# Loading x ahead of the first adjacency rows in a two-layer graph kernel

## The reference

```python
def layer0(x, adj, h0, y):
    a = adj * (y @ y.T)                       # keep an edge only inside a class
    a = a / max(sum(abs(a), axis=1), 1e-12)
    return 0.9 * (a @ x) + 0.1 * h0

def layer1(x, adj, W_proj, b_proj, W_gcn, b_gcn):
    filt = tanh(adj * adj) * (adj > 0)        # tanh(1) at each edge
    a = top_k(filt, 350)                      # no row has over 350 edges
    h2 = tanh(x @ W_proj + b_proj)
    return relu(a @ (h2 @ W_gcn) + b_gcn)

x = layernorm(x + layer0(x, adj, h0, y))
x = layernorm(x + layer1(x, adj, ...))
```

## Time and profile before

| | us |
|---|---|
| median of 3 runs | 468.47 |
| lowest and highest run | 467.95, 468.52 |
| span of the profiled execution, first to last instruction | 465.9 |

### The profile page before, as it was taken

One profiled execution on the slowest core, in us unless ns is written; L12 is line 12 of the kernel. 1 busy time (PEld: TensorE's weight loads), 2 busy tenths in 40 slices (PEclk: granted clock), 3 DMA queues, 4 the chain that ended last, 5 costly groups with the idle time before them and its releaser, 6 DMA issues.

```text
span 465.9 us, 15131 instructions
## 1 busy us (share of the span) xinstructions
PE 438.7 (94%) x5104; PEld 386.3 (83%) x5104; DVE 377.9 (81%) x1359; ACT 263.5 (57%) x355; POOL 161.5 (35%) x310
## 2 busy tenths in 40 slices
PE   3659999999999999999999999999999999999994
PEld 2448898888888988888888887888888888888883
DVE  5988999999999999999999976675575575575562
ACT  4997998999999999999999934900000000000000
POOL 3022543455444455554445541221211211211222
PEclk9977999999999999999999999999999999999998
DMA  8999999999999999999999200000000000000000
GB/s 262 411 414 420 419 417 417 415 408 411 409 422 420 422 423 420 424 423 412 417 419 422 60 2 1 13 11 17 17 11 17 17 11 17 17 11 17 17 11 23
DMA packets 25518, 108.50 MB, mean 233 GB/s; under 512 B 5097, under 2 KB 15490, under 8 KB 15490
## 3 DMA queue, kind: packets, MB, share of 16 engines
q1 hardware_dynamic: 25490, 108.14, 57.5%
HBM read 105.57 MB, written 2.56 MB: 232 GB/s over the span
## 4 chain that ended last, share of the span: by engine, by line
PE 75%; DVE 10%; ACT 5%; issue 5%; DMA 2%; POOL 2%; POOLq 0%; DVEq 0%; ACTq 0%; SPq 0%
PE acc L521 64%; PE words L471 6%; DVE a_bits L783 3%; DMA a_rows<-in_adj_dram 2%; PE feat_acc L584 2%; PE proj_acc L595 2%; ACT count_out L685 2%; DVE turned L870 2%; PE xnt_acc L576 1%; ACT count_out L678 1%; ACT x_parts L664 1%; POOL xs L438 1%; ACT count_out L754 1%; DVE z_high L921 1%; ACT count_out L746 1%
## 5 line engine op out<-in xcount | busy, mean ns | idle before, releaser
L521 PE MATMUL acc<-x_parts,turned 128*128 128x257 f16 (+1 forms) x1600 | 195.2, 276 | 3.2 <-DVE turned L870 1.0
L678 ACT ACTIVATE count_out<-a_rows,ones 128x2688 bf16<-128x2688 f32 (+1 forms) x80 | 190.2, 2377 | 0.5 <-DMA a_rows<-in_adj_dram 0.2
L521 PEld LDWEIGHTS acc<-x_parts,turned 128*128 128x128 fp8e4 (+1 forms) x1600 | 154.4, 98 | 28.9 <-issue 3.8
L521 PE MATMUL acc<-f_parts,turned 128*128 128x256 f16 (+1 forms) x1560 | 171.6, 273 | 0.8 <-DVE turned L870 0.8
L521 PEld LDWEIGHTS acc<-f_parts,turned 128*128 128x128 fp8e4 (+1 forms) x1560 | 152.0, 98 | 19.3 <-issue 1.3
L783 DVE TENSOR_SCALAR a_bits<-a_rows 128x2688 bf16<-128x2688 f32 (+1 forms) x80 | 116.7, 1459 | 2.7 <-DMA a_rows<-in_adj_dram 2.3
L421 POOL TENSOR_TENSOR var_eps<-mean_var,consts 128x1 f32<-128x1 f32 x80 | 18.6, 232 | 266.1 <-DVE mean_var L1077 139.7
L870 DVE TENSOR_SCALAR turned<-a_words 128x320 uint16 (+1 forms) x305 | 66.9, 233 | 53.2 <-PE acc L521 52.8
L424 POOL TENSOR_TENSOR rstd<-var_eps,consts 128x1 f32<-128x1 f32 x80 | 86.5, 1081 | 6.3
L870 DVE TENSOR_SCALAR turned<-same_class 128x320 uint16<-128x320 uint16 x313 | 71.3, 254 | 0.1
L471 PEld LDWEIGHTS words<-pack,a_bits 128*128 128x128 bf16 (+1 forms) x1600 | 51.3, 97 | 9.7 <-DVE a_bits L783 7.8
(11 more groups left out here) (111 smaller groups left out, 288.3 us busy)
## 6 DMA issues: line engine op xcount, KB each, us to landing
a_rows<-in_adj_dram SPq DMA_DIRECT2D x39, 1344.0 KB, 7.8
a_rows<-in_adj_dram SPq DMA_DIRECT2D x39, 1156.0 KB, 8.3
out_dram<-xn SPq DMA_DIRECT2D x39, 64.0 KB, 1.5
h_rows<-in_L_gnn_h_dram SPq DMA_DIRECT2D x19, 128.0 KB, 8.1
xs<-in_x_dram SPq DMA_DIRECT2D x3, 640.0 KB, 10.0
xs<-in_x_dram SPq DMA_DIRECT2D x1, 512.0 KB, 10.3
y_nat<-in_L_gnn_y_dram SPq DMA_DIRECT2D x1, 304.0 KB, 3.6
a_rows<-in_adj_dram SPq DMA_DIRECT2D x1, 84.0 KB
```

Source lines behind the costliest of these rows:

```text
L521: mm = pe.matmul(acc[par][0:m, 0:cols], bits, parts[:, b, 0:cols], start=first and b == blocks[0], stop=last and b == blocks[-1])
L678: act.activation(count_out[0:m, 0:w], a_rows[par][h][0:m, 0:w], ACT.Relu, bias=ones[0:m, 0:1], scale=-HUGE, accum_out=col).then_inc(s_coun ...
```

## The change

SP issues the loads of x ahead of those of block 0's rows. ACT makes `high_part` 0 to 3 ahead of its copies of class words and of block 0's count; `copy_words` of pieces 7 and 9 move behind the second count. DVE makes `low_part` 0 ahead of its `y_diag` copies and 1 to 3 between the copies of class words, ahead of both casts of block 0. No instruction is added or taken away; PE's and POOL's orders stay as they are.

```diff
@@ -350,12 +350,12 @@
             sp.dma_start(y_nat[:, 0, :], y[0:P, :]).then_inc(s_in["y"], 16)
             sp.wait_ge(s_cleared, 1)
             sp.dma_start(y_nat[0:TAIL, FULL, :], y[FULL * P:N, :]).then_inc(s_in["yt"], 16)
-            load_rows(0, 0, 0)
             sp.dma_start(xs[:, 0, :], x[0:P, :]).then_inc(s_in["x0"], 16)
             for q, part in enumerate(X_PART):
                 lo, hi = max(part.start, 1), min(part.stop, FULL)
                 sp.dma_start(pair_view(xs, lo, hi), pairs_of(x, lo, hi)).then_inc(s_in[f"x{q}"], 16)
             sp.dma_start(xs[0:TAIL, FULL, :], x[FULL * P:N, :]).then_inc(s_in["xt"], 16)
+            load_rows(0, 0, 0)
             load_rows(1, 1, 0)
             load_h0(0, 0, 0, 0, 0)
             load_h0(1, 1, 0, 0, 1)
@@ -646,16 +646,6 @@
             act.activation(y2[:, :, C:2 * C], y_nat[:, :, :], ACT.Copy).then_inc(s_y2, 1)
             act.wait_ge(s_packs, 3)
             act.activation(y_masked[:, :, C:2 * C], y_nat[:, :, :], ACT.Copy, scale=row_half[:, 1:2]).then_inc(s_y2, 1)
-            act.wait_ge(s_yt, 2)
-            act.activation(y2_t[:, TURNED * P:2 * TURNED * P], y_turned[1], ACT.Copy).then_inc(s_yt_act, 1)
-            act.wait_ge(s_yp_sb, 1)
-            act.wait_ge(s_yp, 2)
-            for g in range(TURN):
-                act.activation(y_diag[g * 2 * C:(g + 1) * 2 * C, Y_PACK[1], g, :],
-                               y_pack[1].rearrange("p (r w) -> p r w", w=GRAM_W), ACT.Copy).then_inc(s_yp_act, 1)
-
-            def copy_words(g):
-                copy_gram(lambda o, i: act.activation(o, i, ACT.Copy), act, g)
 
             def high_part(q):
                 act.wait_ge(s_in[f"x{q}"], 16 if q else 32)
@@ -664,6 +654,21 @@
                 act.activation(x_parts[:, X_PART[q], 0:F], xs[:, X_PART[q], :], ACT.Copy, scale=SCALE)\
                     .then_inc(s_xhigh, 1)
 
+            high_part(0)
+            act.wait_ge(s_yt, 2)
+            act.activation(y2_t[:, TURNED * P:2 * TURNED * P], y_turned[1], ACT.Copy).then_inc(s_yt_act, 1)
+            high_part(1)
+            act.wait_ge(s_yp_sb, 1)
+            act.wait_ge(s_yp, 2)
+            for g in range(TURN):
+                act.activation(y_diag[g * 2 * C:(g + 1) * 2 * C, Y_PACK[1], g, :],
+                               y_pack[1].rearrange("p (r w) -> p r w", w=GRAM_W), ACT.Copy).then_inc(s_yp_act, 1)
+
+            def copy_words(g):
+                copy_gram(lambda o, i: act.activation(o, i, ACT.Copy), act, g)
+
+            high_part(2)
+            high_part(3)
             for g in range(GRAMS):
                 if not gram_on_dve(g):
                     copy_words(g)
@@ -714,13 +719,7 @@
                     count_zeros(t, par, pair, 0, rows_of(t))
                 if isinstance(t, int) and t == 0:
                     words_of(0, 0)
-                    high_part(0)
-                    high_part(1)
                     copy_words(GRAMS)
-                    high_part(2)
-                    copy_words(GRAMS + 2)
-                    high_part(3)
-                    copy_words(GRAMS + 4)
                 if valid(t - 5):
                     m5 = rows_of(t - 5)
                     act.wait_ge(s_xnt, t - 4)
@@ -729,6 +728,9 @@
                     act.activation(xn_t[:, 0:m5], xnt_acc[:, 0:m5], ACT.Copy).then_inc(s_xnt_sb, 1)
                 if valid(t):
                     count_zeros(t, par, pair, 1, rows_of(t))
+                if isinstance(t, int) and t == 0:
+                    copy_words(GRAMS + 2)
+                    copy_words(GRAMS + 4)
                 if isinstance(t, int) and t == 1:
                     for g in range(2 * GRAMS, 3 * GRAMS):
                         if not gram_on_dve(g):
@@ -791,16 +793,6 @@
             dve.tensor_scalar(y_masked[:, :, 0:C], y_nat[:, :, :], row_half[:, 0:1], None, ALU.mult).then_inc(s_y, 1)
             dve.wait_ge(s_yt, 1)
             dve.tensor_copy(y2_t[:, 0:TURNED * P], y_turned[0]).then_inc(s_yt_dve, 1)
-            dve.wait_ge(s_yp_sb, 1)
-            dve.wait_ge(s_yp, 1)
-            for g in range(TURN):
-                dve.tensor_copy(y_diag[g * 2 * C:(g + 1) * 2 * C, Y_PACK[0], g, :],
-                                y_pack[0].rearrange("p (r w) -> p r w", w=GRAM_W)).then_inc(s_yp_sb, 1)
-
-            cast(0, 0, 0, 0)
-
-            def copy_words(g):
-                copy_gram(dve.tensor_copy, dve, g)
 
             def low_part(q):
                 dve.wait_ge(s_in[f"x{q}"], 16 if q else 32)
@@ -809,6 +801,17 @@
                 dve.wait_ge(s_xhigh, q + 1)
                 dve.scalar_tensor_tensor(x_parts[:, X_PART[q], F:2 * F], xs[:, X_PART[q], :], SCALE,
                                          x_parts[:, X_PART[q], 0:F], ALU.mult, ALU.subtract).then_inc(s_xlow, 1)
+
+            low_part(0)
+            dve.wait_ge(s_yp_sb, 1)
+            dve.wait_ge(s_yp, 1)
+            for g in range(TURN):
+                dve.tensor_copy(y_diag[g * 2 * C:(g + 1) * 2 * C, Y_PACK[0], g, :],
+                                y_pack[0].rearrange("p (r w) -> p r w", w=GRAM_W)).then_inc(s_yp_sb, 1)
+
+
+            def copy_words(g):
+                copy_gram(dve.tensor_copy, dve, g)
 
             def bias():
                 dve.wait_ge(s_bias, 1)
@@ -950,18 +953,18 @@
             def first_step(t, par, pair):
 
                 if t == 0:
+                    low_part(1)
                     copy_words(0)
+                    low_part(2)
                     copy_words(2)
+                    low_part(3)
+                    copy_words(4)
+                    cast(0, 0, 0, 0)
                     cast(0, 0, 0, 1)
-                    copy_words(4)
-                    copy_words(6)
                     mask(0, 0)
                     unpack_block(0, 0)
-                    low_part(0)
-                    low_part(1)
-                    low_part(2)
+                    copy_words(6)
                     copy_words(8)
-                    low_part(3)
                 if t == 1:
                     cast(1, 1, 0, 0)
                     copy_words(10)
```

12 lines of the change are left out of this document (6 added, 6 removed).

## The result

| | median us | lowest to highest | span of the profiled execution |
|---|---|---|---|
| before | 468.48 | 467.95 to 468.52 | 465.9 |
| after | 471.58 | 471.14 to 471.99 | 470.2 |

The change costs 3.1 us: ratio 1.0073, 95% interval 1.0060 to 1.0085. The forecast was 471.5. The two spans differ by more, 4.3 us, and that is where the forecast's working has its fault.

The account below looks back on a forecast made before the run. The DVE and PE chain was taken as the bound, DMA a hair ahead. Product 0 ends 4.1 us late; vanished waits (0.16, 0.27) leave 3.7, swallowed 0.7 leaves 3.0: 468.47 + 3.0 = 471.5 us, range 469.1 to 474.2.

Parts of the forecast that it names:

- What bounds the kernel: Layer 0's loop: the DVE and PE chain sets the pace; its lateness lasts to 262 us unless waits for DMA swallow it.
- Rival C: Layer 0: DMA is the real pacer and the early loss is caught up by the end; no change, 468.5, chance 0.12.
- Start of product 0: Block 0: high part 0 starts at 7.5 us, DVE's list takes 16.3, so product 0 begins at 23.8, 4.1 us later.
- Busy all through: DVE ahead of product 0: it never idles during its list, so waiting less would not make it faster.
- Product 0: 6.1 us forecast: PE at block 0: slow for the first 3.4 us as before, 6.1 us in all, ending at 29.9, 4.1 us late.
- Rival B: PE at product 0: more loss by the clock, slow to its end, 2.5 us more; 474.0, chance 0.13.
- Product 1: 39.4 forecast: PE: product 1 starts at 39.4 in place of 35.76, 3.7 us late, at the slow clock level as before.
- rival A: PE up to product 1: the clock may stay at 2.4 GHz, saving 2.1 us, so +0.9; 469.4, chance 0.15.
- the 1.17 of 3 us of busy time: PE before product 1: small bursts filling 1.17 of 3 us were cited as followed by the 0.50 clock from 30 us.
- 0.7 us of waits are swallowed: 3.7 - 0.7 = 3.0: DVE from 40 to 100 us: two waits, 0.7 us in all, absorb part of the 3.7 us lateness, leaving 3.0.
- DMA may idle for up to 1 us ... I add nothing: Reload of block 3's second half: issued near 33.4, so DMA may idle up to 1 us; the later chain hides it.
- The median lies 2.6 above the span: Sum: before's median lies 2.6 us above its 465.9 span, so the added 3.0 us was put on 468.47.

Follow-up runs that it names:

- the moved reduction: The label test (1.1 us on DVE) moved from step 7 of layer 0 to layer 1: 467.38 us in before (467.72), 471.17 in after.
- the run of 3.0 us at step 11: Before with 12 fills of a spare tile (3.01 us) on DVE behind step 11: 470.85 us against 467.88.
- the loads only: Before with only SP's loads moved (x ahead of block 0's rows), ACT and DVE in their old orders: 474.41 us against 467.88.
- Busy PE in after: After with useless matmuls in PE's gaps before product 0 and up to product 1, to hold the clock: 469.47 us against before's 468.02.
- The early cast: After with DVE's cast of block 1's second half ahead of its copies of class pieces 10 and 12: 469.73 us against before's 467.88.
- the run of 3.0 us at block 0: Before with 12 fills (3.0 us) on DVE ahead of block 0's first cast, no load moved: 470.91 us against 467.92.

## Why the prediction was right, and where it was not

**What bounds the kernel: right.** A lateness at product 8 is there at product 38, within 0.1 us, in every kernel of the table except where 4.6 us of fills were put in at block 0, and where the delay was put in behind block 8. In the kernels with the moved reduction it shifts by up to 0.3 us. Rival C (DMA is the pacer and swallows it) falls with the run of 3.0 us at step 11: DMA had its share of 1.01 in before, and the 3.0 us came out whole. The Trainium skill, "Perfetto Trace Analysis", section "Identifying the Most-Contended Engine", says that occupancy misleads for DMA; the trace agrees, with a share of 1.01 on a resource that was not waited for after 100 us.

**Start of product 0: 23.8 forecast, 24.43 measured.** x landed 7.9 us in, not 7.5, so high part 0 started at 7.94; from there to product 0 the list took 16.5 us, not 16.3. "Busy all through" was not quite true: DVE was idle for 1.62 us before the first low part and 1.44 before the mask, but both stand in the sum as terms of other engines.

**Product 0: 6.1 us forecast, 5.6 measured.** The clock rose earlier against its start than in before. Rival B, product 0 slow to its end, did not happen; with the loads only it nearly did, 7.5 us. Product 0 ended at 30.07; 29.9 was forecast. That is luck in part: a start 0.6 us too early and a duration 0.5 us too long cancel.

**Product 1: 39.4 forecast, 39.34 measured.** All between went as worked out, the slow level included (0.50 from 36 to 40 us), and so rival A's clock gain was not taken. Busy PE in after shows that its mechanism is real and worth 1.65 us. One reading behind it was off: the 1.17 of 3 us of busy time belongs to the stretch from 30 us on, which already ran at the lower level; from 26 to 29 us, ahead of the fall, PE was busy 1.77 of 3 us.

**The step that failed: "0.7 us of waits are swallowed: 3.7 - 0.7 = 3.0", with "DMA may idle for up to 1 us ... I add nothing".** In the profiled execution nothing was swallowed; the lateness went from 3.7 us at products 2 to 5 to 4.1 at product 7 and 4.2 at the end. First, the 0.7 us of waits that were to be swallowed were not on the path. Product 1, slow, had made PE the last of the chain: from there to 70 us PE is busy throughout (the window of before below, with the earlier trace rows), so DVE's waits of 0.38 and 0.27 us before the casts of blocks 5 and 7 delayed no product.

```profile
60.00:70.00 10.00, 10.00 (x138) 1.00 1.02 418
```

Second, the waits for rows grew (1.1 us in place of 0.7), since the stream of rows thinned by 3.3 us, not by at most 1. The prediction saw the one reload that hangs on block 1's second cast (issued 33.60, forecast 33.4, right), and took it as hidden behind a chain that is itself late. But the next reloads wait for late casts, too, and there is little to cover the loss: in before the first halves of blocks 4 and 6 lay ready 0.1 us before their casts (landed 42.24 and 54.98, cast 42.35 and 55.08), and block 5's was waited for. In after block 4's lay ready for 1.9 us, since the chain was late, and by block 6 the thin stream had used that up; block 7's rows then put DVE's cast at 65.57, 4.2 us late, and that is the lateness that stays. The early cast shows it by taking it away, the run of 3.0 us at block 0 by making it without the change. Its size is small beside the rest: 0.4 to 0.5 of the 4.2 us. The bulk, 3.6 us, was there at product 1, as forecast.

**"The median lies 2.6 above the span": wrong.** In every execution whose time and span are both known, the time is 1.7 to 1.9 us over the span; the profiled one of after took 471.99. The profiled execution of before (465.9 + 1.8 = 467.7) was thus 0.8 us under its kernel's median, and the one of after 0.4 over. That is the whole difference between 4.3 us of spans and 3.1 of medians. So the median came out as forecast in part because two errors met, which is luck: 1.3 us too little in the span (3.0 for 4.3), and a base of comparison 0.8 us fast.

How fast that base really was is open. In the later comparisons before's median was 467.72 to 468.02 (7 to 25 executions each), so 467.7 is an ordinary time of this kernel, and the median of the first comparison, 468.48 of four executions, is the high one. Against the later medians after would be 3.6 to 3.9 us slower, but it was not run on those chips.

What makes executions of before differ (467.36 to 469.66 among 25 of them) was not tested. A later rise of the clock in product 0 is not enough: with the delay at step 11, whose order is that of before up to there, the clock rose 0.7 us later than in before, and product 1 still started at 35.67, in before at 35.76. With the reduction moved product 1 started 1.0 us late, and there block 2's rows had landed 1.0 us later, too.

## What to carry to other kernels

In a loop where loads and compute are both full, a delay at the start is carried to the end, and it can grow: ask, for each buffer that is read late, when its reload is issued and how far landing is ahead of use some blocks on. Count a wait as able to swallow a delay only if the engine that ends last stood still in it. An instruction whose input has long landed shouldn't stand behind one that waits for another engine: moving a single cast gave back 1.25 of 3.1 us. And a gain ahead of such a loop is worth only as much as the loads' lead and the other engine allow, so look for it behind the tightest block: a reduction of 1.1 us moved out at block 7 made before 0.3 us faster, just clear of the noise, and 0.8 us faster together with busy PE; 1.85 us won by PE at product 2 alone gave nothing. In the changed kernel the same move gave nothing either.
